# Expert layer of a graph-and-mixture kernel: relu in place in PSUM, halves made from PSUM

## The reference

```python
h = jax.nn.relu(jnp.einsum('td,edh->teh', x_flat, W1) + b1)
y = jnp.einsum('teh,ehd->ted', h, W2) + b2
out = jnp.einsum('ted,te->td', y, combine)
```

## Time and profile before

| | |
|---|---|
| runs | 2301.28 us median of 3 (2299.09 to 2303.33) |
| profiled execution | 2304.95 us, its span 2302.3 us |
| busy over the span | PE 2107.5, DVE 2013.1, POOL 1629.2, ACT 1129.5 us |
| mean granted TensorE clock | 0.968 |

### The profile page before, as it was taken

The page is one execution under the profiler, slowest core; times in us unless marked ns, Lnnn a source line. Parts: engine busy times, 40 slices in busy tenths (PEclk is TensorE's granted clock), DMA queues, the critical chain, the costliest instruction groups (busy, mean ns, idle before and its releaser), DMA issues. The chain is left out here.

```text
span 2302.3 us, 45696 instructions
## 1 busy us (share of the span) xinstructions
PE 2107.5 (92%) x16549; PEld 1852.7 (80%) x16550; DVE 2013.1 (87%) x3390; ACT 1129.5 (49%) x1632; POOL 1629.2 (71%) x1364
## 2 busy tenths in 40 slices
PE   7997789999999999999999999999999449999993
PEld 4665678888888888888888888888799439988993
DVE  7998999999999999999999999998788677676662
ACT  2226655555555555555555545553232247666661
POOL 4770067777777777777777777777777347888873
PEclk9997999999999999999999999999999679999996
DMA  4542433333323333333233333332455534444455
GB/s 141 159 115 74 129 120 91 90 100 93 92 88 101 92 91 92 104 91 92 90 102 90 90 99 93 92 92 85 141 155 155 193 68 74 77 76 78 77 76 139
DMA packets 160928, 235.85 MB, mean 102 GB/s; under 512 B 54834, under 2 KB 121805, under 8 KB 160490
## 3 DMA queue, kind: packets, MB, share of 16 engines
q0 software_dynamic: 70896, 164.43, 28.0%
q1 hardware_dynamic: 75536, 55.29, 8.4%
q10 hardware_dynamic: 14314, 13.68, 1.7%
HBM read 186.46 MB, written 53.24 MB: 104 GB/s over the span
## 5 line engine op out<-in xcount | busy, mean ns | idle before, releaser
L815 POOL DMA_INDIRECT picked<-xn_dram,place x1029 | 1182.3, 1149 | 438.0 <-issue 300.1
L913 PE MATMUL bank<-picked,pick_w 128*128 128x256 f32 x2058 | 504.5, 381 | 15.4 <-DMA picked<-xn_dram,place 14.4
L1025 ACT COPY stage<-bank 128x512 f32<-128x512 f32 x343 | 201.0, 586 | 547.7 <-PE bank L901 545.7
L913 PEld LDWEIGHTS bank<-picked,pick_w 128*128 128x128 f32 x2058 | 387.0, 190 | 83.6 <-issue 32.5
L909 PE MATMUL bank<-window,stage 128*128 128x256 f32 x1568 | 382.9, 387 | 0.0
L1286 DVE TENSOR_TENSOR hot_w<-hots,cur 128x1536 bf16<-128x1536 bf16 x343 | 328.6, 958 | 11.9
L979 ACT COPY field_rep<-fields 128x1666 bf16<-128x1666 bf16 (+1 forms) x193 | 322.5, 1675 | 1.2 <-DVE vals L1162 1.2
L909 PEld LDWEIGHTS bank<-window,stage 128*128 128x128 f32 x1568 | 283.8, 191 | 30.7
L1282 DVE TENSOR_TENSOR hots<-ends,cur 128x1408 bf16<-128x1408 bf16 x343 | 302.5, 882 | 1.7 <-ACT cur L1019 1.7
L901 PE MATMUL bank<-hot_w,hots 128*128 128x128 bf16 x4116 | 286.1, 219 | 4.5 <-issue 3.5
L909 PE MATMUL bank<-stage 128*128 128x256 f32 x1176 | 286.0, 386 | 0.0
(11 more groups left out here) (252 smaller groups left out, 3399.5 us busy)
## 6 DMA issues: line engine op xcount, KB each, us to landing
picked<-xn_dram,place POOLq DMA_INDIRECT x1029
xn_dram<-xn ACTq DMA_DIRECT2D x49, 128.0 KB, 1.9
xT_dram<-xT ACTq DMA_DIRECT2D x49, 128.0 KB, 2.1
base_dram<-acc SPq DMA_DIRECT2D x7, 896.0 KB
sum_dram<-acc SPq DMA_DIRECT2D x7, 896.0 KB
z_dram<-vals SPq DMA_DIRECT2D x7, 896.0 KB, 9.8
out_dram<-sum_dram SPq DMA_DIRECT2D x1, 6250.0 KB, 21.7
acc<-in_x_dram SPq DMA_DIRECT2D x6, 896.0 KB, 5.3
```

Source lines behind the costliest of these rows:

```text
L815: pool.indirect_dma_start(out=picked[:, i % SETS * PICK + q, :], out_offset=None, in_=xn_dram, in_offset=bass.IndirectOffsetOnAxis(ap=plac ...
L913: mm = pe.matmul(sum_ps[pp], pick_w[i % SETS][:, q, :], picked[:, i % SETS * PICK + q, :], start=False, stop=(q == PICK - 1))
L1025: act.copy(block_sb[pp].rearrange("p j c -> p (j c)"), banks[pp][:, :]).then_inc(a_copied, 1)
```

## The change

h is no longer written to SBUF. The relu writes each chunk back to the place in PSUM that it read, `hh` is made by ACT from there, and `hl` by DVE from there and `hh`. The SBUF copy `h` is gone. A new helper, `hid_half`, names one PSUM bank as two chunks. With h gone, the relu no longer waits for `hl_done` of two steps earlier. PE, which overwrites the PSUM chunks two steps later, now waits for that `hl_done` in place of `relu_done`. No instruction changes its place in any engine's order; the only ones gone are the relu's wait and the register operation that counted for it.

```diff
-        h = [acc[:, X + 4 + FC * i:X + 4 + FC * (i + 1), :] for i in range(2)]
...
+        def hid_half(i, m):
+
+            return banks[2 + 2 * i + m][:, :].rearrange("p (c r) -> p c r", c=2)
...
             def relu(j, i, half, e):
                 act.wait_ge(hid, 2 * j + half + 5)
-                act.wait_ge(hl_done, 2 * j + 2)
                 for c in (2 * half, 2 * half + 1):
-                    act.activation(h[i][:, c, :], hid_ps(i, c), ACT.Relu, bias=b1T[:, bass.ds(e * FC + c, 1)]).then_inc(relu_done, 1)
+                    act.activation(hid_ps(i, c), hid_ps(i, c), ACT.Relu, bias=b1T[:, bass.ds(e * FC + c, 1)]).then_inc(relu_done, 1)
 
             def high_h(j, i, half):
                 act.wait_ge(relu_done, 4 * j + 2 * half + 10)
                 act.wait_ge(y_made, j + 1)
-                at = slice(2 * half, 2 * half + 2)
-                act.copy(hh[i][:, at, :], h[i][:, at, :]).then_inc(hh_done, 1)
+                act.copy(hh[i][:, 2 * half:2 * half + 2, :], hid_half(i, half)).then_inc(hh_done, 1)
...
             def hidden(j, i):
                 pe.wait_ge(zl_done, j + 3)
                 pe.wait_ge(wl_done, j + 1)
-                pe.wait_ge(relu_done, 4 * j + 4)
+                pe.wait_ge(hl_done, 2 * j + 2)
...
                     dve.wait_ge(hh_done, 2 * j + half + 1)
                     at = slice(2 * half, 2 * half + 2)
-                    dve.tensor_tensor(hl[i][:, at, :], h[i][:, at, :], hh[i][:, at, :].bitcast(F32), ALU.subtract).then_inc(hl_done, 1)
+                    dve.tensor_tensor(hl[i][:, at, :], hid_half(i, half), hh[i][:, at, :].bitcast(F32), ALU.subtract).then_inc(hl_done, 1)
```

## The result

| | before | changed kernel |
|---|---|---|
| median of 8 runs | 2301.97 us (2299.09 to 2307.41) | 2292.70 us (2286.11 to 2297.29) |
| profiled execution, span | 2304.95, 2302.3 us | 2290.40, 2287.6 us |

A forecast was written before the change was run, and what follows sets the result against it. POOL's end-to-end transfers, lengthened by DVE holds, were taken as the bound. Gains of 5.3 + 5.8 + 0.9 = 12.0 us gave 2292.95 from the profiled 2304.95, or 2289.3 us as a median; own range 2284 to 2292, whole range 2280 to 2300.

The forecast's parts named there:

- The bound: Experts' stage: POOL runs four transfers a step end to end, 6.42 us undisturbed, and bounds the kernel, not PE.
- The hold by two SBUF inputs: A DVE instruction with two SBUF inputs, running 0.1 us after POOL's start, keeps POOL waiting to its end; 18.3 us.
- Term A: First gathers of the 42-step window: 21 holds by `hl` go, 5.3 us gained.
- Term B: Second scatters in the window: `w1l` holds hang on `hl` holds; of 12.8 us, 7 remain, 5.8 us gained.
- The first steps: Seven steps before the window have the same kind of `hl` hold; 0.9 us gained at the same rate.
- The edits at no cost: `hl` and `hh` reading PSUM, relu writing PSUM: lengths like nearest rows or as now, hidden by idle time; 0 us.
- The sum: Whole kernel: 5.3 + 5.8 + 0.9 = 12.0 us gained, median 2289.3 us.
- the rival in which all `w1l` holds stay: Second scatters: as many held by `w1l`, whatever `hl` does; gain 6.2 us, 2295 us; chance 0.14.
- all `w1l` holds go: Second scatters: every hold by `w1l` goes too; gain 19.0 us, 2282 us; chance 0.20.
- `hl` holds as before: First gathers: what holds is not the second SBUF input of `hl`, so no gain, 2301 us; chance 0.11.
- The slower rival: Experts' stage: a beat between `w1l` and second scatter locks all 42 steps; 9.7 us slower, 2311 us; chance 0.05.
- PE: Window: PE does not stop the gain, 6.6 us a step above its 6.15; idle shrinks about as the window does.

The follow-up runs named there:

- e4: Changed kernel with w1l made by two instructions reading PSUM in place of W1 (not W1's low half); 48 steps 308.8 us, ratio 0.9911 to before.
- e1: Changed kernel with hl's first input from an SBUF slice of W1, so hl is not computed; 48 steps 330.6 us, ratio 0.9996 to before.
- e2: Kernel before with hl's first input from PSUM, ahead of bias and relu, and PE waiting for hl_done; 48 steps 318.3 us, ratio 0.9959 to before.
- The three copies: Three profiled executions of the changed kernel, unmodified, in different sets of runs; 48 steps took 318.6, 318.1 and 315.9 us.
- e9: Changed kernel with a memset of 512 columns in front of w1l; 48 steps 325.2 us, ratio 0.9956 to before.

## Why the prediction came out

- *The bound.* Right. POOL's idle time before its transfers did not change by a tenth, and the 42 steps became shorter by as much as POOL's transfers did, 287.6 - 276.9 = 10.7 us against 10.7 us. The prediction's window ends 0.84 us before its last scatter does. That and the 0.3 us to a next transfer are the 1.1 us by which its sum, 269.6 + 18.3 = 287.9, misses 286.8; it took them for roundings. Taking every hold away (e4) gives the 6.43 us a step that the undisturbed step of before promised.
- *The hold by two SBUF inputs.* Shown from both sides: put back, all holds return (e1); done alone, the whole gain is there (e2). The rule of the Trainium skill that the prediction named (SBUF — State Buffer, "SBUF: two separate sides") agrees with both, and with e4. So the engines meet not only at semaphores, as was said at the start. The moment was stated too widely: it is not enough that the instruction runs 0.1 us after POOL's start, since a `w1l` that starts 0.04 us before the scatter up to 0.02 after it holds nothing. The prediction's own row of 2124.81 says so.
- *Term A,* 5.3 us forecast: the gathers lost 89.5 - 84.2 = 5.3.
- *Term B,* 5.8 us forecast by seven remaining holds of 1.0: seven remained, and the scatters lost 147.2 - 141.8 = 5.4. The three copies have 7, 6 and 4; seven was a choice between two counts that contradict each other, and that this trace met it exactly is luck. Its ground, that the `w1l` holds hang on the `hl` holds, is shown by e1 and e2.
- *The first steps,* 0.9 us forecast: from 1906.04 to 1955.01 before, 48.97 us; from 1903.62 to 1951.49 now, 47.87. 1.1 us.
- *The edits at no cost.* `hl` 681 ns, `hh` 587, as their nearest rows had it. The 62 cycles more for a PSUM source in the cost table of the Trainium skill (VectorE: DVE Perf Modes, "The TRN2 errata") do not show here. The relu, which had no row, is 26 ns shorter; e1 and e2 show that this gives nothing. DVE's line 2043, now 2044, still waits for landings, 60.3 us in 42 steps.
- *The sum,* 12.0 us: the 48 steps gave 10.8 between the two profiles, and with the fiftieth step, whose last scatter ends at 2242.64 before and at 2228.29 now, it is 336.60 - 324.67 = 11.9. The medians differ by 9.3 and the profiled executions by 14.6; what is over 11.9 lies outside these 49 steps, 2.4 us of it ahead of them, where the change does nothing that I know of. The measured 2292.7 us is just outside my own range of 2284 to 2292, inside the whole one, and by itself nearer to the rival in which all `w1l` holds stay (2295) than to 2289.3. With runs that spread over 8 to 11 us on each side whole times can't tell them apart; the trace does, with 7 held second scatters in place of 15.
- *The rivals.* The seven holds that stayed rule out that all `w1l` holds go, the eight that went that all stay, and the gathers at 1.02 us over `hl` that `hl` holds as before.
- *The slower rival,* a beat in every step: not seen in any copy of the change. e9 came nearest, 325.2 us, with nine second scatters held by 1.1 to 1.3 us.
- *PE.* Its idle time was to shrink by about as much as the window. It fell from 19.7 to 12.1 us, 7.6 of the 10.7; the other 3.1 are PE's own work, at the higher clock told below.

## What to carry to other kernels

When GpSimd issues indirect transfers end to end, its busy time plus 0.3 us for each transfer is what to compare with the window, and a spread in the length of one and the same transfer is the thing to explain: lay it beside VectorE's order of time. A VectorE subtraction with one input in PSUM cost the same here and let GpSimd through, so an intermediate that is read only by ScalarE and VectorE is better left in PSUM while GpSimd is the bound and the PSUM place is free. Where an instruction with two SBUF inputs can't be avoided, cutting it in two halved its holds; a wait that starts it 0.2 us later removed those of the scatters in one trace, with eight gathers held in their place. How small a shift is enough is not shown.

## What the runs showed that I had not expected

- A memset of 0.11 us, which delays `w1l` by about 0.04 us, took a stage from 316 to 319 us down to 312 to 313, in two traces; beside a `w1l` cut in two, the same delay gave nothing (314.7 and 315.1 us).
- A 0.48 us memset ahead of `w1l` made `w1l` hold scatters that had started up to 0.24 us before its recorded start, for 1.1 to 1.3 us; with `w1l` behind an idle DVE, starts of 0 to 0.25 us after the scatter's held none. So a recorded start is not always the moment from which an instruction keeps others out. What exactly is taken then stays open.
- With fewer holds TensorE's granted clock in the window rose from 0.98 to 1.00, and its busy time fell by 267.91 - 264.82 = 3.1 us for the same steps. It also idled less: it waited for `w1l` 19.6 us in 16 times before (2.1 at the longest), and now (us in all, times, longest us)

```profile
PE bank L1979 <- DVE w1l L2030: 12.1, 12, 1.8
```

That the shorter waits are what raised the clock is not shown.
